# Four result buffers and a down projection three tiles behind in a routed mixture-of-experts layer

## What is computed

```
x = x + tanh(g_xattn) * cross_attention(layernorm(x), ctx, mask)     # 16 heads of 16
h = layernorm(x)
logits = h @ gate_kernel                     # 8 experts, each token takes its best two
y[token] = sum over its two experts e of
             weight(token, e) * ((silu(h @ w0[e]) * (h @ w1[e])) @ wo[e])
x = x + tanh(g_ffn) * y
```

## Time and profile before

| | us |
|---|---|
| median of three runs | 1445.06 |
| the profiled execution | 1446.46 |
| its span | 1444.9 |
| first stage, until the first rows of the second are loaded | about 617 |
| tiles 3 to 21, first `silu` to last | 170.5 |
| tiles 21 to 134, first `silu` to last | 616.4 |

### The profile page before, as it was taken

How to read it: one execution, slowest core, us unless ns; L and a number is a source line. 1 busy time by engine, 2 the same in 40 slices (tenths; PEclk the granted TensorE clock), 3 DMA queues, 4 the chain that set the end, 5 groups by cost and what they waited for, 6 DMA issues and landing times. The chain is left out here.

```text
span 1444.9 us, 36280 instructions
## 1 busy us (share of the span) xinstructions
PE 1235.5 (86%) x9474; PEld 1023.5 (71%) x9475; DVE 954.7 (66%) x2702; ACT 706.5 (49%) x1652; POOL 717.8 (50%) x1134
## 2 busy tenths in 40 slices
PE   4999999999999998176766788888888898888985
PEld 3999999999999997155555566666666666666764
DVE  4888888888888886522222566666566666666673
ACT  3788888888888886021111233333333333333332
POOL 2377777777777776412222344443434444444443
PEclk9999999999999999588888999999999999999998
DMA  5144444444334336557511555555665555555553
GB/s 148 34 144 152 140 147 135 134 136 134 128 128 132 128 132 208 197 182 204 139 28 28 78 99 92 101 101 90 152 112 101 99 93 100 98 98 95 97 96 55
DMA packets 193900, 169.59 MB, mean 117 GB/s; under 512 B 130996, under 2 KB 174548, under 8 KB 191668
## 3 DMA queue, kind: packets, MB, share of 16 engines
q1 hardware_dynamic: 158592, 112.54, 28.2%
q0 software_dynamic: 32064, 52.46, 19.2%
q10 hardware_dynamic: 3188, 3.89, 0.8%
HBM read 68.95 MB, written 70.27 MB: 96 GB/s over the span
## 5 line engine op out<-in xcount | busy, mean ns | idle before, releaser
L1615 PE MATMUL banks<-w_all,etT 128*128 x1620 | 445.8, 412 | 5.6 <-issue 4.5
L1615 PEld LDWEIGHTS banks<-w_all,etT 128*128 128x128 f32 x1620 | 297.7, 196 | 57.1 <-issue 7.1
L605 POOL DMA_INDIRECT out_dram<-ey,eid x135 | 227.6, 1686 | 153.4 <-DVE ey L1321 66.7
L881 ACT ACTIVATE ey<-psB,ewt 128x256 f32<-128x256 f32 x135 | 64.1, 475 | 460.9 <-DMA out_dram<-ey,eid 435.5
L1635 PE MATMUL psB<-w_all,hgT 128*128 x540 | 166.3, 431 | 124.9 <-ACT hgT L867 90.0
L592 POOL DMA_DIRECT2D et<-routed_rows x135 | 78.1, 578 | 375.7 <-issue 375.7
L1635 PEld LDWEIGHTS psB<-w_all,hgT 128*128 128x128 f32 x540 | 96.0, 193 | 189.3 <-issue 178.5
L1321 DVE SCALAR_TENSOR_TENSOR ey<-psB,ewt,ey 128x256 f32<-128x256 f32 x135 | 65.2, 483 | 238.7 <-ACT ey L881 238.1
L1448 PE MATMUL psB<-vbd,probT 128*128 128x51 f32 x1280 | 155.5, 269 | 0.0
L540 POOL DMA_INDIRECT routed_rows<-rows,slot x128 | 126.3, 986 | 57.6 <-DVE slot L1121 29.0
L1448 PEld LDWEIGHTS psB<-vbd,probT 128*128 128x128 f32 x1280 | 152.9, 192 | 0.0
(11 more groups left out here) (177 smaller groups left out, 2354.3 us busy)
## 6 DMA issues: line engine op xcount, KB each, us to landing
split_weights<-w_part SPq DMA_DIRECT2D x16, 1536.0 KB, 6.2
w_all<-split_weights SPq DMA_DIRECT2D x28, 768.0 KB, 4.4
et<-routed_rows POOLq DMA_DIRECT2D x135, 129.0 KB, 2.6
xb<-in_x_dram SPq DMA_DIRECT2D x32, 256.0 KB, 3.4
w_raw<-in_L_ffn_w_kernel_dram SPq DMA_DIRECT2D x32, 256.0 KB
out_dram<-x SPq DMA_DIRECT2D x64, 128.0 KB, 1.8
w_raw<-in_L_ffn_wo_kernel_dram SPq DMA_DIRECT2D x16, 256.0 KB
cb<-in_ctx_dram SPq DMA_DIRECT2D x32, 77.0 KB
```

What stands on the lines that cost most here:

```text
L605: gp.indirect_dma_start(out=out, out_offset=bass.IndirectOffsetOnAxis(ap=eid[:, u % 8:u % 8 + 1], axis=0), in_=ey[:, u % 2, :], in_offset= ...
L1615: m = pe.matmul(banks4[:, bank], etT[:, u % 2, a, c], weight(e, c, w, n), start=(j == 0), stop=(j == len(steps) - 1))
```

## The change

`ey` gets four buffers, and `ewt`, the weights of the rows, eight places. `downs(t)` now names the tiles whose down projection, `y_evac` and `y_sum` belong into tile t: three tiles later for DMA-turned tiles, one tile later for the others, and for the last ones at latest in tile 134. A new list `rounds(t)` keeps the old distances for `high`, `words` and `low`. `y_evac` of tile t waits for the add of tile t-4 in place of t-2. A new list `adds(t)` issues the adds of TensorE-turned tiles two tiles later, in place of four; those of DMA-turned tiles stay at four. TensorE keeps one more expert number over a turn.

```diff
-        ey = sb("ey", [P, 2, D])
+        ey = sb("ey", [P, 4, D])
-        ewt = sb("ewt", [P, 4])
+        ewt = sb("ewt", [P, 8])
...
+        LAG = 3
+
         def downs(t):
+
+            if not isinstance(t, int):
+                return [LAG]
+            out = []
+            for d in range(max(0, t - LAG), t):
+                runs = d + 1 if on_pe(d) else min(d + LAG, MOE_T - 1)
+                if runs == t:
+                    out.append(t - d)
+            return out
+
+        def rounds(t):
 
             out = []
             if known(t, 2) and not on_pe(t - 2):
                 out.append(2)
             if known(t, 1) and on_pe(t - 1):
                 out.append(1)
+            return out
+
+        def adds(t):
+
+            out = []
+            if known(t, 4) and not on_pe(t - 4):
+                out.append(4)
+            if known(t, 2) and on_pe(t - 2):
+                out.append(2)
             return out
...
-                                      in_=ey[:, u % 2, :], ...
+                                      in_=ey[:, u % 4, :], ...
...
                 if below(t, MOE_T - 2):
                     load_rows(t + 2, u + 2)
-                if known(t, 4):
-                    if not known(t, 5):
-                        gp.wait_ge(tab_done, 2)
-                    add_rows(t - 4, u - 4, q)
+                if not known(t, 1):
+                    gp.wait_ge(tab_done, 2)
+                for lag in adds(t):
+                    add_rows(t - lag, u - lag, q)
...
             def y_evac(t, u, q):
                 act.wait_ge(ey_ps, t + 1)
-                if known(t, 2):
-                    act.wait_ge(added[u % 2], 16 * (q * (TURN // 2) + u // 2))
-                act.activation(ey[:, u % 2], psB[:, D:2 * D], ACT.Copy, scale=ewt[:, u % 4:u % 4 + 1]).then_inc(ey_low, 1)
+                if known(t, 4):
+                    act.wait_ge(added[u % 2], 16 * (q * (TURN // 2) + u // 2 - 1))
+                act.activation(ey[:, u % 4], psB[:, D:2 * D], ACT.Copy, scale=ewt[:, u % 8:u % 8 + 1]).then_inc(ey_low, 1)
...
-                if isinstance(t, int) and t == HALF_UP + 2:
+                if isinstance(t, int) and t == HALF_UP + LAG:
                     fetch_last_down()
                 silu(t, u)
-                for lag in downs(t):
+                for lag in rounds(t):
...
             def tile(t, u, q):
-                for lag in downs(t):
+                for lag in rounds(t):
```

More of the change, by code:

```diff
@@ L605, in add_rows @@
                 gp.indirect_dma_start(out=out, out_offset=bass.IndirectOffsetOnAxis(ap=eid[:, u % 8:u % 8 + 1], axis=0),
-                                      in_=ey[:, u % 2, :], in_offset=None, compute_op=ALU.add).then_inc(added[u % 2], 16)
+                                      in_=ey[:, u % 4, :], in_offset=None, compute_op=ALU.add).then_inc(added[u % 2], 16)
             gp.wait_ge(tab_done, 1)
@@ L1315, in e_low @@
                 dve.tensor_copy(eid[:, u % 8:u % 8 + 1], et[:, u % 2, D:D + 1]).then_inc(eid_done, 1)
-                dve.tensor_copy(ewt[:, u % 4:u % 4 + 1], et[:, u % 2, D + 1:D + 2]).then_inc(eid_done, 1)
+                dve.tensor_copy(ewt[:, u % 8:u % 8 + 1], et[:, u % 2, D + 1:D + 2]).then_inc(eid_done, 1)
             def y_sum(t, u):
                 dve.wait_ge(ey_low, t + 1)
-                dve.scalar_tensor_tensor(out=ey[:, u % 2], in0=psB[:, 0:D], scalar=ewt[:, u % 4:u % 4 + 1], in1=ey[:, u % 2],
+                dve.scalar_tensor_tensor(out=ey[:, u % 4], in0=psB[:, 0:D], scalar=ewt[:, u % 8:u % 8 + 1], in1=ey[:, u % 4],
                                          op0=ALU.mult, op1=ALU.add).then_inc(ey_done, 1)
@@ L1648, in _ @@
             expert, weights_need = {}, {}
-            carried = {n: pe.alloc_register(f"expert_{n}") for n in ("next", "last", "second_last")}
+            carried = {n: pe.alloc_register(f"expert_{n}") for n in ("next", "last", "second_last", "third_last")}
             carried_need = pe.alloc_register("weights_need")
@@ L1655, in tile @@
                     if known(t, 1):
-                        expert[0], expert[-1], expert[-2] = (pe.snap(r, min_val=0, max_val=SLOTS - 1) for r in carried.values())
+                        expert[0], expert[-1], expert[-2], expert[-3] = (pe.snap(r, min_val=0, max_val=SLOTS - 1) for r in carried.values())
                         weights_need[0] = pe.snap(carried_need, min_val=2 * 16 * DC, max_val=2 * 16 * NQ)
@@ L1673, in tile @@
                         pe.reg_mov(carried["second_last"], expert[u - 1])
+                        pe.reg_mov(carried["third_last"], expert[u - 2])
                 if known(t, 1) and on_pe(t - 1):
```

## The result

The changed kernel takes 1302.45 us (median of 4 runs, 1301.03 to 1307.34), beside 1445.84 for the kernel before on the same chip: a ratio of 0.9007 [0.8974, 0.9041]. The forecast was 1264, so 38 us of the expected gain did not come; the time lies inside the range of 1247 to 1306, near its upper end, and outside the 1247 to 1281 that the prediction gave its own mechanism.

A forecast was written before the change was run, and what follows sets the result against it. The prediction took the ring of `y_evac` waiting for adds into the output to bound the kernel, with no engine full. From 1446.46 us, -83.2 (first tiles), -105.0 (tiles 21 to 134) and +5.9 (end) gave 1264, range 1247 to 1306.

The forecast's parts named there:

- the prediction's own mechanism: Behind tile 21: TensorE bounds at 4.40 to 4.70 us a tile, giving 1247 to 1281 us; chance 0.66.
- part 1: Expert stage: with four buffers `y_evac` waits for the add four tiles back, and that wait goes to zero.
- the same ring: Expert stage: `y_evac` waits for an earlier add's landing; 9.2 us per TensorE-turned tile, 10.7 per two DMA-turned tiles.
- Part 2: Tiles 3 to 21: 18 steps of 4.85 us, 87.3 us in place of 170.5, so -83.2 us.
- Part 3: Tiles 21 to 134: TensorE bounds at 4.55 us a tile, 511.4 in place of 616.4, -105.0 us (-122.0 to 0).
- The register moves at a turn: Loop turns: a few short instructions on queues that run ahead, counted as costing nothing.
- The three tiles of slack: Last weight fetch on ScalarE, moved by a tile: the slack covers what it delays, counted as costing nothing.
- the transpose ring: DMA-turned tiles: `halves`, transpose, landing L, `words`, next `halves` take 4.16 + L over two tiles; binds from L = 4.64.
- The rival on transposes: Behind tile 21: landing L sets the pace; 1296 us at 5.5, 1341 at 6.3, chance 0.12; 1477 at 8.7 (slower, 0.01).
- Part 4: After the last `up`: one more add, +4.65, and `high` waiting for `down`, 1.3; +5.9 us, between +3 and +8.
- VectorE's (1288): Behind tile 21: `words` and `halves` both meet adds, 4.76 a tile, chance 0.14; with long port block 1426 us, 0.01.
- 750 + 113 p: Whole kernel: its time in us, where p is the pace per tile behind tile 21, forecast 4.55.

The follow-up runs named there:

- the kernel with two reads: The changed kernel without TensorE's third register read per tile, its weight wait folded into the wait before the up projection: 1268.3 us, ratio 0.8749.
- the kernel with both edits: The changed kernel without the third register read per tile and with the last expert's weights fetched one load per tile: 1259.91 us, ratio 0.8689.

## Why the prediction was right, and where it was wrong

The direction and the two large gains came as forecast. That the time lies inside the range is in part luck. The range reached up to 1306 to take in two rivals that did not happen; the prediction's own mechanism was given 1247 to 1281, and the two costs that made up the difference it had counted as nothing or nearly so.

**What bounds the kernel before, and part 1: right.** The wait for an add went from 435.5 us in 122 runs to none that shows. It is over-determined, though: each of four buffers, the third tile and (in the first tiles) early adds does it alone. The prediction gave the buffers the whole effect and did not say that the third tile cuts the same ring. It gave the third tile the end of TensorE's wait for `high`, and that went with the buffers alone.

**Part 2, the first tiles: right to 0.3 us**, 87.6 for 87.3. A step seen in the trace of before with the buffer free was the right row.

**Part 3, the pace behind tile 21: wrong by +35.4 us**, and the whole miss. The failed step is "TensorE's own step is seen where nothing held it", 4.40 us, taken with 3.4% on top as 4.55. It was 4.84. The 4.40 was true of that one step, and the kernel with two reads runs 4.45 in its loops: matmuls allow it. What the step did not show is TensorE's queue. Its third read took 300 ns there; the source line in the trace of before says how unlike the rest that is, first around the step of the earlier trace rows (1065 to 1073 us), then over the stretch:

```profile
L1629 PEldq TENSOR_LOAD <-tdown_i x2: 300/300/301, 1066.3 to 1072.2; - x2
...
L1629 PEldq TENSOR_LOAD <-tdown_i x111: 297/396/797, 815.3 to 1418.3; - x111
```

While the ring held the kernel at 5.455 a tile, the idle time could hide a read of 0.8 us; at 4.5 it can't, as the run with two reads shows. "The register moves at a turn are a few short instructions on queues that run ahead" is the same mistake in words: TensorE's queue did not run ahead. The tiles at a loop turn take 5.25 us in the changed kernel and the others 4.70, and 4.46 with two reads, where the queue has time again.

**"The three tiles of slack cover what the fetch delays": wrong, +11.6 us of the 35.4.** The slack lies between adds and `y_evac`. By the prediction's own sum for the transpose ring, 2 x 4.55 - 4.16, a landing has about 4.9 us. The kernel before shows the cost already, and the prediction put it into its 3.4%: the same seven steps took 45.0 us there, where seven steps of its loop pace of 5.41 are 37.9. The rival on transposes had this mechanism, with L = 8.7 at the far end, but as a state of each tile; L was 13.7 once and 3.4 in the median.

**Part 4, the end: right.** The last `up` ends at 1273.3, the last add starts at 1291.80, 18.5 us behind it for a forecast of near 19. The timeline, which answers to the earlier trace rows:

```profile
1271.68 1.64 PE L1637 MATMUL banks<-w_all,etT 128*128 x6
...
1277.93 1.55 POOL L627 DMA_INDIRECT out_dram<-ey,eid  x1 [4.44 <-DVE ey L1343]
1282.55 1.54 POOL L627 DMA_INDIRECT out_dram<-ey,eid  x1 [3.06 <-DMA out_dram<-ey,eid]
...
1291.80 1.55 POOL L627 DMA_INDIRECT out_dram<-ey,eid  x1 [3.12 <-DMA out_dram<-ey,eid]
```

**The rivals.** VectorE did not become the bound, with or without a lock of the port. `words` rose from a mean of 754 ns to 774, and its median from 744 ns to 747, far from the 900 in the median that would have spoken for it:

```profile
L1329 DVE COPY hT<-hT 128x1024 uint16<-128x1024 uint16 x112 | 86.6, 774 | 13.5 <-DMA hT<-hs 12.3 <-issue 0.2
```

Those 12.3 us of waiting for a transpose in 112 tiles, most of it 7.4 once at the fetch, also settle the transpose ring. The DMA's share did rise as forecast, to 0.66, but the landing that this was to lengthen stayed at 3.4 us in the median for 3.5. The time of the transpose rival (1296) and of VectorE's (1288) happen to lie near the measured one; neither mechanism is what happened. In the sum 750 + 113 p, the pace of the kernel with both edits, (506.14 + 2.8) / 113 = 4.504, gives 1259, and it takes 1259.91. The arithmetic held (that the whole agrees to 1 us is partly chance, as single terms are off by about as much); p was sized from the engines and not from the queue that feeds them.

## What to carry to other kernels

When a wait is cut and an engine becomes the bound, look at its queue too: count register reads, register operations and waits per tile, which no busy share shows, and compare their lengths in the step used as a model with their median. Two remedies for one ring don't add, so try each alone; and judge a deeper pipeline only after the next bound is gone, since the third tile looked worthless with three reads and was worth 9 us net with two. The bursts of a fetch show in the trace of the kernel before, so price them there as a term of their own. A bulk fetch in the middle of a steady loop is worth spreading over tiles.

## What the runs showed of the hardware that was not expected

- A read of one number from SBUF into a register by TensorE's sequencer takes 295 to 300 ns at the shortest, about 0.6 us in the median in the slower stretches, and up to 1.07 us (1.14 with four reads per tile). Moving it to another place of the tile brought it from 594 to 300 ns in the median, without any gain in time.
- The third such read in a tile, with its register operations and its wait, costs 0.31 us where the tile takes 4.45 without it, and the fourth 0.63.
- A DMA transpose that takes 3.4 us in the median took 13.7 beside four weight transfers issued in 2.5 us, and 8.0 at most with these spread over tiles.
- The clock's mean over the first tiles rose from 0.86 to 1.00 when the gaps went (87.62 of 87.64 us busy, from 104.70 of 159.23).
